# Four indirect row scatters of a batch, issued as two pairs or one by one across two iterations

## The chip, the cores and the metric

The kernel runs on one core of one Trainium2 chip. The metric is the device time of an execution in microseconds; the time before is the median of three runs. One further execution was recorded by the hardware profiler, and the rows shown come from it.

## The reference

One transformer block with adaptive layer norm, for 32 batches of 256 tokens and 128 features: attention with 8 heads, then a mixture of 8 experts of which each token takes 2. Cut to what matters:

```python
h = layernorm(x) * (1 + ca) + sa
x = x + ga * attn(h)            # q, k: rmsnorm and rope; causal softmax; 8 heads of 128
h = layernorm(x) * (1 + cb) + sb
scores = softmax(h @ Wr + br)
_, top_idx = top_k(scores, 2)   # weights: softmax over the chosen two
expert_out = gelu(h @ W1[e] + b1[e]) @ W2[e] + b2[e]
x = x + gb * sum over the two chosen e of weights[e] * expert_out[e]
```

All inputs and outputs are float32.

## The kernel before

The kernel has two stages. In the first, attention and the choice of experts, a software pipeline goes over the 32 batches; in the second the rows of the tokens, sorted by expert in DRAM (`x_rows`), are taken in tiles through the experts' matrices, and their results go back by rows (`y_rows`). Between the stages stand the ends of one block of instruction streams and the start of another.

In the first stage each engine has one written-out stream, `body(half, parity, live)`, called by `iterations` for n = -2 to 33. The iterations n = 8 to 29 are a loop of 11 turns with two iterations in each (parity 0 and 1); those before and after are unrolled. Iteration n works on several batches at once, each at its own step: the layer norm of batch n + 1 (flag X), queries and keys of batch n (A), their transposes and the values of batch n - 1 (B), scores, softmax and values times probabilities of batch n - 2 (C), the gated residual of batch n - 3 (R), the second layer norm of batch n - 4 (N2), the logits and choice of experts of batch n - 5 (RT), and the places and scatters of batch n - 6 (ST). Each engine goes through eight head groups h = 0 to 7, a half of one of four 128 x 1024 products each.

For a head group TensorE (from L1133 on) makes the scores of one head (L1162 to L1165), the product that gives queries or keys (L1129), at h = 0, 1, 5 and 6 eight transposes of an earlier product (L1204), at h = 2 and 3 the values (L1129 again), and then values times probabilities of the head before (L1144 to L1147). The transposes at h = 5 and 6 take the scaled queries; they share one PSUM tensor, UN[1], so those at h = 6 wait until ScalarE has copied those of h = 5 to `q_t` (L733). ScalarE does the exponentials of a head (L690, L692), four squares with sums of the product (L714), which wait for the product, and copies. VectorE divides and adds the heads (L966, L982), multiplies the product by cosine (L1015) and sine (`rope_b`, L1030), and for h = 0 to 3 adds the two (L1039). At h = 3 it sums the places (L950), and at h = 4 it copies the turned rows of batch n - 5 into `rows` (L960), for which it waits until the scatters of batch n - 7, which read the same buffer, have landed.

GpSimd's stream is in the order of the function below: `roots`, `gated_residual`, `newton`, `offsets`, `scale_queries(0)`, the product `place_k`, `scale_queries(1)`, scatter of row tile 0 (two indirect DMAs, one for each chosen expert), the scores of RT, scatter of row tile 1 (two more), `h_lo`, the second weight, and the sums `add(4)` to `add(7)` with small steps of RT between them. An indirect DMA writes 128 rows of 129 float32 values to `x_rows` at the rows that `place` names. `alone` is a wait of its own instruction; in the loop, where its value is not constant, it is a move to a register and two waits.

`rows` and `place` have two buffers each, by the parity of the batch. Batch 27 (LAST - 1) is scattered in the second stage (L1414). SP's stream waits for the scatters of batches 0 to 26 (L426) before it issues the loads of the first three tiles (L430).

Of the kernel before, what the change touches and what calls it, by code (L numbers as in the profile page):

```python
# [19 lines left out]
def adaln_block(nc, x, wq, wk, wv, wo, wr, br, w1, b1, w2, b2, c, wmod, rope_cos, rope_sin, out):  # L20
# [12 lines left out]
    K = 2  # L33
# [13 lines left out]
    LAST = NB - LATE  # L47
# [12 lines left out]
    with ctx:  # L60
# [27 lines left out]
        x_rows = nc.dram_tensor("x_rows", [(E * REGION + SPARE * TILE), RW], F32).ap()  # L88
# [114 lines left out]
        rows = [sb("rows0", [P, K, TT, RW]), rows_kept]  # L203
# [27 lines left out]
        place = [sb("place0", [P, TT * K], I32), place_kept]  # L231
# [203 lines left out]
        def _(pool):  # L435
# [50 lines left out]
            def body(half, parity, live):  # L486
# [79 lines left out]

                def scatter(t):

                    b = n - 6
                    alone(pool, "place_ready", b + 1)  # L570
                    alone(pool, "rows_tagged", b + 1)
                    for j in range(K):
                        at = place[parity][:, t * K + j:t * K + j + 1]
                        pool.indirect_dma_start(  # L574
                            out=x_rows, out_offset=bass.IndirectOffsetOnAxis(ap=at, axis=0),
                            in_=rows[parity][:, j, t, :], in_offset=None).then_inc(S[f"scattered{parity}"], 16)

                if X or A or B or C or R or N2:
                    roots()
                if R:  # L580
                    gated_residual()
                if X or A or B or C or R or N2:
                    newton()
                    offsets()
                if B:
                    scale_queries(0)
# [7 lines left out]
                if B:  # L594
                    scale_queries(1)
                now = ST and not (isinstance(n, int) and n - 6 == LAST - 1)
                if now:
                    scatter(0)
                if RT:
# [4 lines left out]
                                       op=ALU.mult).then_inc(S["scored"], 1)  # L604
                if now:
                    scatter(1)
                if X:
                    b = n + 1
                    wait(pool, "hhi_done", b + 1)
                    wait(pool, "vw_done", TT * (b - 1))  # L610
                    pool.tensor_tensor(out=h_lo[other][:, :], in0=h_t[:, :], in1=h_hi[other][:, :], op=ALU.subtract)\
                        .then_inc(S["h_ready"], 1)
                if ST:
                    b = n - 6
# [5 lines left out]
                if A:  # L620
                    add(4)
                    add(5)
# [1379 lines left out]
```

## Time and profile before

| | us |
|---|---|
| median of 3 runs | 1255.39 |
| lowest and highest | 1252.91, 1262.49 |
| profiled execution | 1272.64 |
| its span, first to last instruction | 1270.7 |

The span is what the profile's rows are measured in: their times are microseconds from its start. Busy times of engines are parts of it. The profiled execution is one run, a little over the range of the three timed ones, so a sum of rows is a sum for that execution, and the median is a second reference. An idle time in square brackets stands before an instruction, with what ended it.

### The profile page before, as it was taken

To read this page: it belongs to the slowest core of one execution; us is meant where nothing else is said; L and a number is where in the kernel's file an instruction comes from. 1 tells how busy PE (TensorE), PEld (TensorE's weight loads), DVE (VectorE), ACT (ScalarE), POOL (GpSimd) and SP (SyncE) were. 2 spreads that over 40 slices of the span, in tenths; PEclk is the share of its full clock that TensorE was granted. 3 is DMA by queue.
4 is the path that set the end of the run, shared out by engine and by line. 5 is a ranking of instruction groups with operands and counts; after the bars stand their busy time and mean duration, and the time that the engine had idled before them with its cause. 6 is when DMAs were issued, how large, how long until landed. Compare 5 with 4: busy or idle time off the path is not lost. (4 is left out here: it accounts for less than half of the span.)

```text
span 1270.7 us, 30656 instructions
## 1 busy us (share of the span) xinstructions
PE 1068.5 (84%) x7431; PEld 805.2 (63%) x7431; DVE 941.6 (74%) x2589; ACT 976.5 (77%) x3518; POOL 791.5 (62%) x1198
## 2 busy tenths in 40 slices
PE   3699999999898899989999998999899679887700
PEld 2278888777777777767777776787654334566500
DVE  2988888888887787878778787887567466565644
ACT  3889998888888887878888787887598458776532
POOL 2556577767666676666667666677446656654543
PEclk9999999999999999999999999999999879998855
DMA  8300000000000000000000000000333232210064
GB/s 261 112 19 5 4 12 12 14 12 19 11 11 11 12 12 11 15 15 11 11 12 12 11 15 15 11 12 16 98 98 93 69 97 80 82 53 23 32 247 150
DMA packets 50769, 57.73 MB, mean 45 GB/s; under 512 B 7868, under 2 KB 38703, under 8 KB 50644
## 3 DMA queue, kind: packets, MB, share of 16 engines
q1 hardware_dynamic: 33492, 35.37, 9.3%
q0 software_dynamic: 8704, 16.87, 4.0%
q10 hardware_dynamic: 8448, 4.20, 1.1%
q14 instruction: 92, 0.75, 0.2%
q8 instruction: 33, 0.54, 0.2%
HBM read 33.21 MB, written 24.23 MB: 45 GB/s over the span
## 5 line engine op out<-in xcount | busy, mean ns | idle before, releaser
L714 ACT ACTIVATE squares<-unit 128x128 f32<-128x128 f32 x1024 | 270.3, 290 | 37.2 <-remote 25.2
L1444 POOL DMA_INDIRECT y_rows<-y_out,place_y x144 | 153.9, 1069 | 121.5 <-DVE y_out L1826 77.2
L714 ACT ACTIVATION_READ_ACCUMULATOR squares<-unit 128x1 f32 x1024 | 226.3, 223 | 0.0
L544 POOL TENSOR_TENSOR roped<-roped,rope_b 128x512 f32<-128x512 f32 x128 | 165.6, 1294 | 97.3 <-DVE rope_b L1030 95.2
L1015 DVE TENSOR_TENSOR roped<-unit,cos_sb 128x512 f32<-128x512 f32 x256 | 175.0, 684 | 57.2 <-ACT squares L714 53.8
L690 ACT ACTIVATE probs<-scores,rr 128x256 f32<-128x256 f32 x256 | 121.5, 475 | 85.2 <-PE scores L1165 53.0
L1204 PE MATMUL unit<-ident,roped 128*128 128x128 f32 x1024 | 139.2, 280 | 53.8 <-ACT q_t L733 39.0
L1204 PEld LDWEIGHTS unit<-ident,roped 128*128 128x128 f32 x1024 | 115.6, 142 | 100.0 <-issue 83.3
L1030 DVE TENSOR_TENSOR rope_b<-unit,sin_sb 128x512 f32<-128x512 f32 x256 | 173.5, 678 | 0.0
L574 POOL DMA_INDIRECT x_rows<-rows,place x108 | 109.9, 1018 | 64.2 <-DVE place L950 42.1
L1039 DVE TENSOR_TENSOR roped<-roped,rope_b 128x512 f32<-128x512 f32 x128 | 141.9, 1109 | 4.4
L982 DVE SCALAR_TENSOR_TENSOR acc<-pv,den,acc 128x128 f32<-128x128 f32 x448 | 135.8, 338 | 0.3
L1531 ACT ACTIVATE hidden<-up,b_t 128x512 f32<-128x512 f32 (+1 forms) x188 | 100.1, 597 | 34.2 <-remote 20.7
L552 POOL TENSOR_TENSOR roped<-roped,rr 128x1024 f32<-128x1024 f32 x64 | 122.0, 1910 | 0.0
L966 DVE RECIPROCAL den<-pv 128x2 f32<-128x2 f32 x256 | 40.5, 158 | 100.3 <-PE pv L1147 62.4
L1129 PE MATMUL unit<-wqk_hi,h_hi 128*128 128x512 f16 x256 | 100.6, 393 | 10.3 <-DVE rope_b L1030 8.4
L1144 PE MATMUL pv<-vals,probs 128*128 128x129 f32 x512 | 104.0, 285 | 0.1
L1129 PE MATMUL unit<-wqk_lo,h_hi 128*128 128x512 f16 x256 | 100.8, 394 | 0.0
L1129 PE MATMUL unit<-wqk_hi,h_lo 128*128 128x512 f16 x256 | 100.3, 392 | 0.0
L1162 PE MATMUL scores<-q_t,k_t 128*128 128x128 f32 x512 | 99.6, 276 | 0.5 <-ACT q_t L733 0.5
L1147 PE MATMUL pv<-vals,probs 128*128 128x129 f32 x512 | 99.8, 277 | 0.0
L1164 PE MATMUL scores<-q_t,k_t 128*128 128x128 f32 x512 | 99.7, 277 | 0.0
(292 smaller groups left out, 3010.9 us busy)
## 6 DMA issues: line engine op xcount, KB each, us to landing
shared<-y_rows SPq DMA_DIRECT2D x16, 512.0 KB, 5.2
x_all<-in_L_attn_x SPq DMA_DIRECT2D x32, 128.0 KB, 2.1
out_x<-sums ACTq DMA_DIRECT2D x16, 256.0 KB, 3.9
rope_b<-x_rows SPq DMA_DIRECT2D x13, 258.0 KB
tile_x<-x_rows SPq DMA_DIRECT2D x12, 258.0 KB
y_rows<-y_out,place_y POOLq DMA_INDIRECT x144
x_rows<-filler SPq DMA_DIRECT2D x16, 129.0 KB
k_t<-in_L_ffn_W SPq DMA_DIRECT2D x2, 1024.0 KB, 10.1
```

The source lines that it names most:

```text
L544: pool.tensor_tensor(out=roped[parity][:, u, heads], in0=roped[parity][:, u, heads], in1=rope_b[:, u % 2, heads], op=ALU.add).then_inc(S[" ...
L552: pool.tensor_tensor(out=v, in0=v, in1=r, op=ALU.mult).then_inc(S["qs_done"], 1)
L574: pool.indirect_dma_start(out=x_rows, out_offset=bass.IndirectOffsetOnAxis(ap=at, axis=0), in_=rows[parity][:, j, t, :], in_offset=None).t ...
L690: nc.scalar.activation(probs[:, h % NPR, 0:T], SC[h % 2][:, 0:T], ACT.Exp, scale=r[:, kc:kc + 1]).then_inc(S["exp_done"], 1)
L714: nc.scalar.activation(squares[:, c * D:(c + 1) * D], UN[0][:, c * D:(c + 1) * D], ACT.Square, accum_out=ssq[parity][:, u * H + c:u * H + ...
L982: ins = nc.vector.scalar_tensor_tensor(out=a[:, t, :], in0=o[:, t, 0:M], scalar=den[:, h % 2, t:t + 1], in1=a[:, t, :], op0=ALU.mult, op1= ...
L1015: nc.vector.tensor_tensor(out=roped[parity][:, u, heads].rearrange("p (g c) -> p g c", c=D // 2), in0=UN[0][:, heads].rearrange("p (g c) - ...
L1030: nc.vector.tensor_tensor(out=rope_b[:, u % 2, heads].rearrange("p (h s c) -> p h s c", h=HH, s=2), in0=UN[0][:, heads].rearrange("p (h s ...
L1039: nc.vector.tensor_tensor(out=roped[parity][:, u, heads], in0=roped[parity][:, u, heads], in1=rope_b[:, u % 2, heads], op=ALU.add).then_in ...
L1129: ins = nc.tensor.matmul(dst[:, k:k + 512], a, w[:, k:k + 512], start=(m == 0), stop=(m == 2))
L1204: ins = nc.tensor.transpose(UN[1][:, j * P:(j + 1) * P], roped[other][:, u, j * D:(j + 1) * D], ident[:, :])
L1444: pool.indirect_dma_start(out=y_rows, out_offset=bass.IndirectOffsetOnAxis(ap=place_y[i % (2 * SLOTS)][:, s:s + 1], axis=0), in_=y_out[at] ...
```

## The change

In GpSimd's stream of the first stage, `scatter` issues one indirect DMA instead of two, and takes the batch, its buffer, the row tile and the expert's number. The four scatters of batch b = n - 6 now stand at four places: the first where the first pair stood, the second behind `add(4)`, the third first in iteration n + 1, ahead of `roots`, and the fourth in iteration n + 1 behind `offsets`. Each has its own pair of waits. `add(4)` comes before the second weight. The number of scatters, what they write and their semaphores' final counts stay. For batch 26 the last two are issued in n = 33.

```diff
-                def scatter(t):
-
-                    b = n - 6
+                def scatter(b, k, t, j):
+
                     alone(pool, "place_ready", b + 1)
                     alone(pool, "rows_tagged", b + 1)
-                    for j in range(K):
-                        at = place[parity][:, t * K + j:t * K + j + 1]
-                        pool.indirect_dma_start(
-                            out=x_rows, out_offset=bass.IndirectOffsetOnAxis(ap=at, axis=0),
-                            in_=rows[parity][:, j, t, :], in_offset=None).then_inc(S[f"scattered{parity}"], 16)
-
+                    at = place[k][:, t * K + j:t * K + j + 1]
+                    pool.indirect_dma_start(
+                        out=x_rows, out_offset=bass.IndirectOffsetOnAxis(ap=at, axis=0),
+                        in_=rows[k][:, j, t, :], in_offset=None).then_inc(S[f"scattered{k}"], 16)
+
+                now = ST and not (isinstance(n, int) and n - 6 == LAST - 1)
+                rest = not isinstance(n, int) or 0 <= n - 7 < LAST - 1
+                if rest:
+                    scatter(n - 7, other, 1, 0)
                 if X or A or B or C or R or N2:
                     roots()
...
                     newton()
                     offsets()
+                if rest:
+                    scatter(n - 7, other, 1, 1)
                 if B:
                     scale_queries(0)
...
                     scale_queries(1)
-                now = ST and not (isinstance(n, int) and n - 6 == LAST - 1)
                 if now:
-                    scatter(0)
+                    scatter(n - 6, parity, 0, 0)
                 if RT:
...
-                if now:
-                    scatter(1)
                 if X:
...
+                if A:
+                    add(4)
+                if now:
+                    scatter(n - 6, parity, 0, 1)
                 if ST:
...
                 if A:
-                    add(4)
                     add(5)
```

## Rows read from the trace of the kernel before

**Rows 1.** The page, busy time and share of the span: TensorE's multiplications.

```profile
PE 1068.5 (84%) x7431; PEld 805.2 (63%) x7431; DVE 941.6 (74%) x2589; ACT 976.5 (77%) x3518; POOL 791.5 (62%) x1198
```

**Rows 2.** Busy time by stretch: length, each engine's busy (instructions), granted clock, DMA share, GB/s.

```profile
143.43:168.12 24.69, 24.69 (x187) 20.34 (x187) 21.78 (x66) 22.74 (x97) 14.99 (x27) 1.00 0.02 5
193.07:217.89 24.82, 24.82 (x189) 20.16 (x188) 21.99 (x70) 22.56 (x98) 18.81 (x32) 1.00 0.05 16
606.53:634.39 27.86, 25.27 (x189) 20.10 (x188) 22.71 (x70) 23.89 (x103) 18.87 (x33) 1.00 0.04 12
634.39:661.27 26.88, 25.20 (x189) 20.11 (x188) 22.50 (x69) 22.09 (x93) 18.87 (x33) 1.00 0.04 13
217.89:828.72 610.83, 559.46 (x4116) 446.10 (x4115) 496.64 (x1519) 506.42 (x2135) 414.91 (x684) 0.99 0.04 13
```

**Rows 3.** Groups of instructions, the loop: count, busy us, mean ns, idle before, what ended it.

```profile
L1039 DVE TENSOR_TENSOR roped<-roped,rope_b 128x512 f32<-128x512 f32 x88 | 98.7, 1122 | 3.0
L1204 PE MATMUL unit<-ident,roped 128*128 128x128 f32 x704 | 94.6, 277 | 51.4 <-ACT q_t L733 39.0 <-ACT k_t L733 11.4
L574 POOL DMA_INDIRECT x_rows<-rows,place x88 | 89.9, 1022 | 54.4 <-DVE place L950 37.4 <-issue 17.0
```

**Rows 4.** Order of time, loop iteration n = 22: start, duration, engine, instruction, idle before.

```profile
619.56 1.04 POOL L574 DMA_INDIRECT x_rows<-rows,place  x1 [1.64 <-DVE place L950]
619.75 0.67 DVE L1030 TENSOR_TENSOR rope_b<-unit,sin_sb 128x512 f32<-128x512 f32 x1
620.90 1.07 POOL L574 DMA_INDIRECT x_rows<-rows,place  x1 [0.30 <-issue]
621.49 0.38 PE L1129 MATMUL unit<-wqk_hi,h_lo 128*128 128x512 f16 x1
622.39 1.01 POOL L574 DMA_INDIRECT x_rows<-rows,place  x1 [0.17 <-issue]
623.71 0.96 POOL L574 DMA_INDIRECT x_rows<-rows,place  x1 [0.30 <-issue]
623.99 0.28 ACT L714 ACTIVATE squares<-unit 128x128 f32<-128x128 f32 x1 [1.52 <-remote]
624.69 0.68 POOL L611 TENSOR_TENSOR h_lo<-h_t,h_hi 128x256 f16<-128x256 f32 x1
626.67 1.09 PE L1204 MATMUL unit<-ident,roped 128*128 128x128 f32 x8 [1.61 <-ACT q_t L733]
```

**Rows 5.** Order of time, unrolled iteration n = 7, GpSimd's scatters and ScalarE's squares.

```profile
204.23 1.04 POOL L574 DMA_INDIRECT x_rows<-rows,place  x1 [0.99 <-DVE place L950]
205.57 0.96 POOL L574 DMA_INDIRECT x_rows<-rows,place  x1 [0.30 <-issue]
207.33 1.01 POOL L574 DMA_INDIRECT x_rows<-rows,place  x1 [0.49 <-issue]
207.72 0.28 ACT L714 ACTIVATE squares<-unit 128x128 f32<-128x128 f32 x1
208.64 0.96 POOL L574 DMA_INDIRECT x_rows<-rows,place  x1 [0.30 <-issue]
```

**Rows 6.** Order of time, loop iteration n = 23: GpSimd, VectorE and ScalarE before the scatters.

```profile
638.22 0.25 POOL L516 TENSOR_TENSOR correction<-guess 128x40 f32<-128x40 f32 x1 [0.68 <-ACT guess L741]
639.97 1.90 POOL L552 TENSOR_TENSOR roped<-roped,rr 128x1024 f32<-128x1024 f32 x1
640.35 2.06 DVE L1039 TENSOR_TENSOR roped<-roped,rope_b 128x512 f32<-128x512 f32 x1
641.62 0.87 ACT L761 ACTIVATE xn<-x_all,off,rr 128x128 f32 x2
645.36 0.16 DVE L950 TENSOR_REDUCE place<-place_k 128x4 int32<-128x32 f32 x1
```

**Rows 7.** Order of time, the end of the first stage: SP's first tile loads, TensorE.

```profile
898.65 2.02 SPq L430 DMA_DIRECT2D rope_b<-x_rows  x3
911.98 0.63 PE L1930 MATMUL xt<-ident,rope_b 128*128 128x128 f32 x4 [2.33 <-PEq L1288]
```

## What the change will do to the time

> **What bounds the kernel now.** I read the page first: TensorE is busy 1068.5 us of the span [rows 1], the most of any engine, and little of it is idle between 60 and 900 us, where attention runs. All the changed code runs there. So the second view is busy time by stretch, cut at GpSimd's first instruction of an iteration (L496) [rows 2]. The reader is to see three lengths. An iteration without scatters takes 24.69 us and TensorE is busy for all of it. The unrolled iteration n = 7, with the same four scatters as the loop's, takes 24.82 and TensorE is again busy throughout. The loop's two iterations take 27.86 and 26.88, with TensorE idle for 2.59 and 1.68. The 22 iterations of the loop take 610.83 us, 27.77 each, and TensorE is idle for 51.4 of them. So the loop is not bound by work: about 3 us an iteration go into a wait.
>
> The groups of instructions in the loop name it [rows 3]: all 51.4 us of idleness stand before the transposes of L1204, 39.0 of it until ScalarE has copied q_t, 11.4 until k_t. The k_t part is at the loop's jump (10 times, only before even n). The q_t part comes in each iteration, 39.0 / 22 = 1.77 us.
>
> The order of time shows where it starts [rows 4]. The product of head group 5 ends on TensorE at 621.49 + 0.38 = 621.87, but ScalarE's squares of it begin at 623.99, after 1.52 us idle "remote", that is, on a signal that came later than the record of the work. The late squares delay the copy of q_t, and TensorE stands for 1.61 us until 626.67. In just these 5 us GpSimd runs its four scatters: starts 619.56, 620.90 (1.34 apart), 622.39, 623.71. In the unrolled iteration [rows 5] the starts are 204.23, 205.57, 207.33, 208.64: the second pair begins 1.76 after the second scatter instead of 1.49, and the squares follow their product without idle time. My reading: while GpSimd issues scatters one upon another, TensorE's signals are held back; where a pause lies between them, the hold ends soon and is hidden. That is an inference from where the idle time lies, not a row.
>
> **The change, part by part.** It adds and removes no scatter: 22 x 4 = 88 in the loop [rows 3], about 1.02 us each, and the rows move the same bytes. It places them (A) first in the iteration, (B) behind offsets, both for the batch before, (C) where the first stood, (D) behind add(4).
>
> (1) The burst goes. Starts become some 6 us apart: A at about 0.2, B at 6.5, C at 12 to 13, D at 17 to 18 us of an iteration. Worth at most the whole q_t wait, 39.0 us; at least nothing, if a lone scatter holds a signal as long.
>
> (2) A before roots. One scatter and its gap, 1.04 + 0.30 = 1.34 us [rows 4], up to 1.8 if its waits are not passed early. It waits for nothing (its batch's rows and places are an iteration old). Behind it stand roots, L560, L565 and newton; in [rows 6] newton begins at 638.22, with 0.68 us of idle time in front of it, so rr and the offsets come 0.5 to 1.1 us later. The scaling at 639.97 begins when they are done; ScalarE wants them for xn at 641.62, 1.6 us on: nothing on the path.
>
> (3) B before scale_queries(0). The scalings, 1.90 us each, start 1.3 to 2.7 us later than at 639.97 in [rows 6], the second ends near 12.5 us of the iteration. TensorE takes the first scaled queries with the transposes of head group 5, at 14 us: hidden, cover 1.5 us or more. place_k slides between the scalings to about 10.5 us; VectorE sums places at 645.36, which is 10.97: cover 0.3 us, the thinnest.
>
> (4) Three pairs of waits more on GpSimd's queue. In the loop the first scatter starts 0.9 us after VectorE's sum of places ended, so one set costs up to 0.75 us where nothing hides it. GpSimd's work is 18.9 us [rows 2]; with four scatter gaps of up to 0.75 it needs 22, under 24.8. After scatter D it does add(5) at 19.3, and add(7) still waits for VectorE. Hidden, but no longer loosely.
>
> (5) h_lo and score come forward: h_lo stood at 624.69 [rows 4] behind four scatters, now behind one. No reader waits for it this early: nothing.
>
> (6) The last two scatters move to n = 33, where B ends near 903. The first tile loads, issued at 898.65 [rows 7], wait for all scatters and go out 6 us later; TensorE's first transpose of a tile is at 911.98, so these loads have some 6 us of cover for the time they need. Nothing; without cover it would be once, not per iteration.
>
> (7) VectorE's sums collide elsewhere with the scalings. L1039 has a mean of 1122 ns in the loop [rows 3] and took 2.06 us at 640.35, beside the scaling of 639.97 to 641.87 [rows 6]: it ended only after it. With B first, this sum is free (1.4 us gained on VectorE, which TensorE does not need), but the next one, now due near 10 us, may meet the second scaling. If it does, the following rope_b slips by up to 1.4 us; its cover is the start of the product of head group 5, 621.49 - 2 x 0.21 = 621.07, less 619.75 + 0.67, that is 0.65 us [rows 4]. Price 0 to 0.8 us an iteration; at four chances in ten I take 0.3.
> The Trainium skill (SBUF — State Buffer, section "SBUF: two separate sides") says why: a VectorE tensor_tensor with both inputs in SBUF and a GpSimd operation exclude each other for the whole instruction; the row agrees.
>
> Sum for an iteration of the loop: 1.77 gained, 0.3 lost, 1.47; by 22, 32 us. The unrolled iterations have nothing to gain, TensorE being full there. The profiled execution took 1272.64 us (span 1270.7) and goes to about 1240. The median of the runs shown, 1255.39, is 17 us lower; the 39 us of waits cannot all be the profiler's then, and I take the same 32 off: 1223.
>
> **Rivals.** (a) Nothing moves. The late signals have another source, or are much shorter in a timed run. For: GpSimd is shown by no row as the releaser; the difference between profiled and timed is of the same order as the waits. Against: [rows 5] has the same work without the wait. Time 1252 to 1259. Chance 0.17.
> By the same section of the skill, TensorE and ScalarE never wait on another engine's or a DMA's access to SBUF; the late signals would then not be the scatters', and the time 1255. The rows show only that they coincide.
>
> (b) The signals improve but VectorE's collision takes most of it: 0.8 to 1.4 us of the 1.77 is lost again. Gain 8 to 21 us, time 1234 to 1247. For: cover 0.65. Against: VectorE begins that stretch 1.4 us earlier. Chance 0.10.
>
> (c) Slower. A lone scatter holds TensorE's signals as long as one in the burst, and there are now four places instead of one; B falls where ScalarE copies vals right after its product. If two of the four cost ScalarE the 1.52 us of [rows 4], that is 3.04 for 1.77: 1.27 x 22 = 28 us, time 1283 (1268 to 1290). It decides once a lone scatter costs the path more than 1.77 / 4 = 0.44 us. For: each scatter's transfer and issue are as before. Against: in [rows 5] four of them, in two pairs, cost TensorE nothing. Chance 0.13.
>
> **How the numbers follow.** The forecast has 0.60: 1223, and its own range is 1255 less the full 39 and some of the jump's 11, that is 1208, up to 1236. Adding (b) and (a) reaches 1260; (c) is left out with some of the lowest end. Range 1207 to 1260. About 1%, 12.5 us, is what a measurement can tell from no change: below 1243 lie the forecast and two thirds of (b), 0.67; within, (a) and the rest of (b), 0.20; above, 0.13.
>
> **What would show it.** In the profile after: loop iterations of 25 to 26.5 us; before L1204 at most 10 us until q_t in all, the k_t part as before; "remote" gone before squares (L714) and den; GpSimd's four scatters 5 us or more apart; L1039's longest cases in other head groups. The sum is wrong if q_t waits stay with scatters apart (a), if they turn into waits of TensorE for rope_b (b), or if new late signals stand beside A, B or D (c).

## The result and the profile after

The changed kernel is faster by about half of what was forecast. Its median is 1245.43 us over 8 runs, against 1261.26 us over 8 runs of the kernel before: a ratio of 0.9889, 95% interval 0.9854 to 0.9924, or 16 us. The forecast was 32 us, to 1223. (The kernel before has a median of 1258 to 1264 us on the chips used below, so each ratio is taken with the runs beside it.)

The profiled execution took 1243.83 us, against 1272.64 before. That difference of 28.8 us is two things, which the table parts. The first stage ends here where TensorE begins the first tile's transpose [rows 7]; the loop is cut at TensorE's first scores of n = 8 and of n = 30. (The windows of [rows 2] and of the stretches below are cut at GpSimd's L496, which comes 1.3 us later against TensorE in after, with a scatter ahead of it. The loop's length is the same within 0.1 us by either cut.)

| profiled execution, us | before | after | difference |
|---|---|---|---|
| first stage up to the loop (n = 8) | 214.7 | 215.4 | +0.7 |
| the 22 iterations of the loop | 610.8 | 588.2 | -22.6 |
| from the loop to the first tile | 86.4 | 90.5 | +4.1 |
| first stage | 912.0 | 894.1 | -17.9 |
| second stage | 358.7 | 347.8 | -10.9 |

No changed line runs in the second stage, and in the twelve profiles of this study it took 346.6 to 358.7 us, with before and after near the two ends. The 10.9 us are its own spread. The 17.9 us of the first stage are what the change did, and they agree with the 16 us timed.

Busy time by stretch, kernel after (length, then each engine's busy time and instructions in the order TensorE, its weight loads, VectorE, ScalarE, GpSimd, then the granted clock, DMA share, GB/s). The stretches are n = 7, n = 22, n = 23, the loop, and the second stage:

```profile
194.10:219.90 25.80, 25.04 (x188) 19.99 (x187) 22.36 (x70) 22.89 (x98) 19.08 (x32) 1.00 0.05 15
594.20:621.30 27.10, 25.70 (x191) 20.66 (x192) 23.86 (x73) 23.92 (x102) 19.02 (x32) 1.00 0.04 12
621.30:647.50 26.20, 24.77 (x185) 19.71 (x183) 22.09 (x67) 22.08 (x95) 18.96 (x31) 1.00 0.05 14
219.72:807.98 588.26, 557.95 (x4119) 447.03 (x4118) 503.24 (x1519) 507.96 (x2136) 418.32 (x683) 0.99 0.04 13
894.10:1241.90 347.80, 239.30 (x1456) 150.46 (x1456) 212.43 (x411) 226.61 (x398) 197.42 (x186) 0.85 0.32 99
```

Against [rows 2], the loop is 22.6 us shorter. TensorE's idle time there fell from 51.4 to 588.26 - 557.95 = 30.3 us, which is 21.1 of it. But the unrolled n = 7 is 1.0 us longer, where nothing had been waited for before.

Groups of instructions in the loop of after:

```profile
L1043 DVE TENSOR_TENSOR roped<-roped,rope_b 128x512 f32<-128x512 f32 x88 | 106.9, 1215 | 3.0
L1208 PE MATMUL unit<-ident,roped 128*128 128x128 f32 x709 | 94.2, 276 | 23.3 <-DVE rows L964 11.3 <-ACT k_t L737 11.1
L1133 PE MATMUL unit<-wqk_hi,h_hi 128*128 128x512 f16 x176 | 67.4, 383 | 7.0 <-DVE rope_b L1034 7.0
```

Lines from `scatter` on stand up to four further down in the changed file: L1208, L1133, L1043 and L964 are L1204, L1129, L1039 and L960 of before. In [rows 3] TensorE's transposes waited 39.0 us for ScalarE's q_t. That wait is gone altogether. Two waits for VectorE stand in its place: 11.3 us until it has copied `rows` (L964), and 7.0 until it has written `rope_b` (L1034), together 18.3. The wait for k_t at the loop's jump is as before, 11.1 beside 11.4.

In order of time, iteration n = 22 of after (compare [rows 4, 6]):

```profile
593.11 1.01 POOL L572 DMA_INDIRECT x_rows<-rows,place  x1 [0.18 <-issue]
600.13 1.23 POOL L572 DMA_INDIRECT x_rows<-rows,place  x1 [0.65 <-issue]
601.40 1.90 POOL L552 TENSOR_TENSOR roped<-roped,rr 128x1024 f32<-128x1024 f32 x1
603.03 2.88 DVE L1043 TENSOR_TENSOR roped<-roped,rope_b 128x512 f32<-128x512 f32 x1
603.25 0.25 POOL L595 TENSOR_TENSOR place_k<-one_hot,place_e 128x32 f32<-128x32 f32 x1
603.46 1.90 POOL L552 TENSOR_TENSOR roped<-roped,rr 128x1024 f32<-128x1024 f32 x1
606.99 1.01 POOL L572 DMA_INDIRECT x_rows<-rows,place  x1 [1.64 <-DVE place L954]
607.92 0.39 PE L1133 MATMUL unit<-wqk_hi,h_hi 128*128 128x512 f16 x1 [0.35 <-DVE rope_b L1034]
608.58 0.67 DVE L964 COPY rows<-unit 128x512 f32<-128x512 f32 x1
609.31 1.09 PE L1208 MATMUL unit<-ident,roped 128*128 128x128 f32 x8 [0.57 <-DVE rows L964]
612.53 1.01 POOL L572 DMA_INDIRECT x_rows<-rows,place  x1 [0.16 <-issue]
```

The four scatters are 5.5 to 7 us apart, and no signal comes late beside any of them: where VectorE waits for a product beside a scatter, `den` starts 0.04 us behind the product's end, as elsewhere. The second one pushes the two scalings (L552) to 601.40 and 603.46. VectorE's sum of head group 2 starts at 603.03 and ends at 605.91, 0.55 us after the second scaling has ended: 2.88 us, where a sum of the same shape takes 0.69 us undisturbed. Everything that VectorE does next is late, `rope_b` and then the copy of `rows`, and TensorE stands 0.35 us for the one and 0.57 for the other.

### The profile page after: what moved, and what is told of

Read it like the earlier page. It is cut to its first block and busy times, and to the rows that moved or that the text cites. A ratio compares the mean times of both kernels' runs of the same rounds, so it can differ in the third digit from the quotient of the medians.

```text
span 1241.9 us, 30842 instructions
## 1 busy us (share of the span) xinstructions
PE 1061.9 (86%) x7431; PEld 805.2 (65%) x7431; DVE 951.8 (77%) x2589; ACT 979.0 (79%) x3518; POOL 797.9 (64%) x1198
## 5 line engine op out<-in xcount | busy, mean ns | idle before, releaser
L544 POOL TENSOR_TENSOR roped<-roped,rope_b 128x512 f32<-128x512 f32 x128 | 166.1, 1297 | 100.8 <-DVE rope_b L1034 99.0
L718 ACT ACTIVATION_READ_ACCUMULATOR squares<-unit 128x1 f32 x1024 | 222.8, 219 | 0.0
L1034 DVE TENSOR_TENSOR rope_b<-unit,sin_sb 128x512 f32<-128x512 f32 x256 | 173.6, 678 | 0.0
L1208 PE MATMUL unit<-ident,roped 128*128 128x128 f32 x1024 | 138.0, 279 | 27.5 <-DVE rows L964 13.8
L1208 PEld LDWEIGHTS unit<-ident,roped 128*128 128x128 f32 x1024 | 117.2, 142 | 68.3 <-DVE rows L964 25.8
L1043 DVE TENSOR_TENSOR roped<-roped,rope_b 128x512 f32<-128x512 f32 x128 | 150.8, 1178 | 4.4
L552 POOL TENSOR_TENSOR roped<-roped,rr 128x1024 f32<-128x1024 f32 x64 | 122.1, 1911 | 0.8
L1133 PE MATMUL unit<-wqk_hi,h_hi 128*128 128x512 f16 x256 | 100.2, 391 | 18.6 <-DVE rope_b L1034 16.6
L1148 PE MATMUL pv<-vals,probs 128*128 128x129 f32 x512 | 104.1, 285 | 0.1
L1133 PE MATMUL unit<-wqk_lo,h_hi 128*128 128x512 f16 x256 | 100.0, 391 | 0.0
L1133 PE MATMUL unit<-wqk_hi,h_lo 128*128 128x512 f16 x256 | 99.7, 389 | 0.0
L1151 PE MATMUL pv<-vals,probs 128*128 128x129 f32 x512 | 99.5, 276 | 0.0
L1149 PE MATMUL pv<-vals,probs 128*128 128x129 f32 x512 | 99.5, 276 | 0.0
```

Source lines behind the costliest of these rows:

```text
L544: pool.tensor_tensor(out=roped[parity][:, u, heads], in0=roped[parity][:, u, heads], in1=rope_b[:, u % 2, heads], op=ALU.add).then_inc(S[" ...
L552: pool.tensor_tensor(out=v, in0=v, in1=r, op=ALU.mult).then_inc(S["qs_done"], 1)
L718: nc.scalar.activation(squares[:, c * D:(c + 1) * D], UN[0][:, c * D:(c + 1) * D], ACT.Square, accum_out=ssq[parity][:, u * H + c:u * H + ...
L1034: nc.vector.tensor_tensor(out=rope_b[:, u % 2, heads].rearrange("p (h s c) -> p h s c", h=HH, s=2), in0=UN[0][:, heads].rearrange("p (h s ...
L1043: nc.vector.tensor_tensor(out=roped[parity][:, u, heads], in0=roped[parity][:, u, heads], in1=rope_b[:, u % 2, heads], op=ALU.add).then_in ...
L1133: ins = nc.tensor.matmul(dst[:, k:k + 512], a, w[:, k:k + 512], start=(m == 0), stop=(m == 2))
```

## The experiments

The theory tested: the q_t wait comes from the burst of scatters, and half of what its removal gives is taken back by the second scatter, which stands ahead of the scalings and makes VectorE's sum meet them. The rivals: the q_t wait is the profiler's or another cause's; and what is lost comes from the first or fourth scatter, or from batches' scatters reaching into the next iteration. Each sum below is of the loop's 22 iterations, n = 8 to 29, in the profile.

### All four in their own iteration

From after: the third and fourth scatters stand behind `add(5)` and ahead of `add(7)` of their batch's iteration.

```diff
-                if rest:
-                    scatter(n - 7, other, 1, 0)
                 if X or A or B or C or R or N2:
...
-                if rest:
-                    scatter(n - 7, other, 1, 1)
                 if B:
                     scale_queries(0)
...
                     add(5)
+                if now:
+                    scatter(n - 6, parity, 1, 0)
...
+                if now:
+                    scatter(n - 6, parity, 1, 1)
                 if A:
                     add(7)
```

> All four scatters one by one, but all in their own iteration: where the first pair stood, behind add(4), behind add(5), behind the counts ahead of add(7). Nothing stands before the query scalings. Theory 1 (the scatters' burst held TensorE's signals back, and in the changed kernel the shifted scalings blocked VectorE's sum at head group 2): no idle time before the transposes until q_t and none until the rows' copy, L1043's counterpart at about 2 us at most, loop iterations of 24.8 to 26, that is 25.7 on average (26.74 in the changed kernel, 27.77 before), a span about 20 us under the changed kernel's. Rival (TensorE's waits of the changed kernel come from scatters as such, wherever they stand): about 0.9 us per iteration stay, loop iterations of 26.7. Timed: theory 1 1220 to 1232, rival 1243 to 1250.

Measured: 1223.88 us against 1258.36, ratio 0.9700 (0.9642 to 0.9757). The loop and its transposes:

```profile
215.61:786.20 570.59, 551.94 (x4117) 445.37 (x4116) 491.25 (x1519) 504.36 (x2135) 416.45 (x683) 1.00 0.04 14
L1207 PE MATMUL unit<-ident,roped 128*128 128x128 f32 x704 | 93.6, 276 | 18.7 <-ACT k_t L736 10.9 <-POOL roped L544 7.7
```

The loop is 17.7 us shorter than in after. No `rows` and no q_t wait is left. A new one, 7.7 us for GpSimd's sum of an earlier product (L544), shows that GpSimd's later work is not free either; two scatters now stand ahead of its last sum, which is the likely reason. So scatters apart are worth the forecast's gain and more, as long as none stands ahead of the scalings.

### The second pair behind `h_lo`

From before: both pairs stay whole, and only one 0.68-us instruction is put between them.

```diff
-                if now:
-                    scatter(1)
                 if X:
...
                         .then_inc(S["h_ready"], 1)
+                if now:
+                    scatter(1)
```

> The kernel before with one step moved: the low part of the layer norm (0.68 us) stands between the two pairs of scatters instead of behind them, so the second pair starts later after the first. Theory 1 (a third scatter on the heels of the second prolongs the hold): the wait for q_t before the transposes, 39.0 us in the loop, falls under 8 us and a loop iteration takes 25.7 to 26 us, as nothing else was moved. Rival (the place in the iteration decides, not the spacing): it stays at 35 to 40 us and 27.7 us an iteration. Timed: 1225 to 1235 against 1250 to 1262.

Measured: 1228.67 us against 1258.36, ratio 0.9761 (0.9713 to 0.9808).

```profile
214.88:785.60 570.72, 557.66 (x4117) 444.00 (x4115) 493.01 (x1519) 506.01 (x2135) 413.83 (x683) 1.00 0.05 14
L1204 PE MATMUL unit<-ident,roped 128*128 128x128 f32 x704 | 93.6, 276 | 10.2 <-ACT k_t L733 9.2
619.54 1.09 POOL L574 DMA_INDIRECT x_rows<-rows,place  x1 [0.30 <-issue]
621.66 1.01 POOL L574 DMA_INDIRECT x_rows<-rows,place  x1 [0.17 <-issue]
```

The last two lines are the second and third scatter of an iteration: 2.12 us from start to start, where the kernel before had 1.49 [rows 4]. That alone ends the q_t wait, 39.0 us to none, with the four still begun within 4.8 us. The loop gains 40.1 us and the timed median 29.7. Nothing has to be set apart one by one, and nothing moved to the next iteration. The late signals are not all gone: in each iteration ScalarE's exponentials of a head, beside the second pair, start 0.7 to 0.8 us behind the end of their scores, where 0.2 is usual. TensorE does not wait for them here.

### The next iteration's second scatter behind the scalings

From after: one scatter moves by two scalings and `place_k`.

```diff
                     offsets()
-                if rest:
-                    scatter(n - 7, other, 1, 1)
                 if B:
                     scale_queries(0)
...
                     scale_queries(1)
+                if rest:
+                    scatter(n - 7, other, 1, 1)
                 if now:
```

> The changed kernel with one of its scatters moved: the one behind the offsets stands behind the second query scaling, so that the scalings start 1.3 to 2 us earlier. Theory 1: VectorE's sum at head group 2 falls from 2.88 us to about 1, TensorE's waits for the rows' copy (13.0 us between 200 and 870) and for rope_b before the product (7.6 us) fall under 5 us together, loop iterations lose about 0.9 us (26.74 to 25.8). That scatter then stands 1.4 to 2 us ahead of the next, a pair; if pairs hold signals too, up to 0.6 us of this is not seen. Rival (these waits come from the scatter first in the iteration): unchanged.

Measured: 1230.07 us, one execution, against 1258.36. The loop, its transposes, and VectorE's sum of head group 2 in an iteration:

```profile
215.50:783.05 567.55, 552.87 (x4116) 445.31 (x4115) 493.31 (x1519) 503.64 (x2135) 422.61 (x683) 1.00 0.04 14
L1208 PE MATMUL unit<-ident,roped 128*128 128x128 f32 x704 | 93.6, 276 | 14.7 <-ACT k_t L737 11.0 <-DVE rows L964 2.6
614.77 0.99 DVE L1043 TENSOR_TENSOR roped<-roped,rope_b 128x512 f32<-128x512 f32 x1
```

This is the run that decides the place of the loss. The scatter ahead of `roots` and the one behind `add(4)` stayed where the change put them, and the loop fell by 20.7 us against after. The sum takes 0.99 us instead of 2.88, the wait for `rows` 2.6 us instead of 11.3, and the wait for `rope_b` is gone. It also has two scatters next to each other, behind the scalings, and no q_t wait.

### The second pair behind `add(4)`

From before: the pair moves further, past `h_lo`, the second weight and `add(4)`.

```diff
                     add(4)
+                if now:
+                    scatter(1)
+                if A:
                     add(5)
```

> The kernel before with its second pair of scatters behind add(4), 4 us or more after the first pair. Theory 1, in its narrow form (it takes a third scatter on the heels of the second): no wait for q_t, loop iterations of 25.7 to 26. In its wide form (any second scatter on the heels of a first holds signals for 1.5 us): 20 us or more of waits until q_t or of late signals stay in the loop, 26.5 us and more an iteration.

Measured: 1238.33 us, one execution, against 1258.36. From the loop's windows and its waits (us in total, times, longest):

```profile
216.75:791.38 574.63, 555.69 (x4117) 445.76 (x4116) 488.90 (x1519) 505.62 (x2135) 415.14 (x683) 1.00 0.04 14
PE pv L1145 <- DVE acc L983: 13.8, 22, 0.7
```

Again no q_t wait. But the 574.6 us are 26.1 an iteration, a little over the narrow form's range, and TensorE waits 13.8 us for VectorE's `acc` in a place where the other kernels have no such wait. The order of time shows why:

```profile
604.71 0.39 PE L1148 MATMUL pv<-vals,probs 128*128 128x129 f32 x2
604.91 0.96 POOL L574 DMA_INDIRECT x_rows<-rows,place  x1 [0.30 <-issue]
606.40 0.17 DVE L967 RECIPROCAL den<-pv 128x2 f32<-128x2 f32 x1 [1.58 <-PE pv L1148]
608.04 0.46 PE L1145 MATMUL pv<-vals,probs 128*128 128x129 f32 x2 [0.63 <-DVE acc L983]
```

The product ends on TensorE at 604.71 + 0.39 = 605.10. VectorE, idle for it, begins `den` at 606.40, 1.3 us later, while the pair's second scatter runs; `acc` and TensorE follow late. In all 22 iterations this `den` starts 1.24 to 1.34 us behind its product. So a pair of scatters 1.3 us apart holds signals too, for a shorter time than four in a row, and at this place TensorE's path needs one of them. The expectation's wide form is right in that and wrong on the size, and its narrow form, that it takes a third scatter, falls.

### All four in a row behind `h_lo`

From before: the burst is not parted but moved.

```diff
                         .then_inc(S["h_ready"], 1)
+                if now:
+                    scatter(0)
+                if now:
+                    scatter(1)
```

> The kernel before with all four scatters behind the layer norm's low part, 1.34 us apart throughout, some 2.5 us later in the iteration. Theory 1 (three and more scatters on each other's heels hold TensorE's signals back wherever they stand): late signals again, 20 us and more in the loop of idle time until a signal later than its work's record, now at head groups 5 to 7; loop iterations of 26.5 us and more. Rival (the place in the iteration decides): none, and 25.7 to 26 us.

Measured: 1307.76 us, one execution, against 1264.05: the slowest kernel of the study. The loop's window, and three of its waits (us in total, times, longest):

```profile
218.98:859.72 640.74, 575.43 (x4116) 458.80 (x4115) 492.10 (x1521) 502.00 (x2135) 411.64 (x683) 0.97 0.04 12
PE unit L1244 <- ACT q_t L733: 59.1, 22, 2.8
DVE den L966 <- remote: 52.8, 22, 2.6
ACT probs L690 <- remote: 44.0, 17, 2.9
```

The four start 1.26 to 1.34 us apart. The late signals ("remote") moved with them, from the squares of head group 5 to later readers of TensorE's products, on VectorE and on ScalarE alike, and the longest are 2.6 to 2.9 us. With the same four DMAs of the same rows in each iteration, the loop takes 570.7 us with 2.12 us in the middle of them and 640.7 with 1.3 throughout. That ties the long late signals to the burst: they went with it to another place, and a pause in its middle takes them away. Not all of the 70 us are waits. TensorE's idle time went from 13.1 to 65.3 us, and its own busy time from 557.7 to 575.4, at a mean granted clock of 0.97 beside 1.00.

### `place_k` ahead of both scalings

From the version with the second pair behind `h_lo`: the scalings start late, as in after, but through `place_k` and not through a scatter.

```diff
                     offsets()
-                if B:
-                    scale_queries(0)
                 if ST:
                     b = n - 6
...
                                        op=ALU.mult).then_inc(S["place_k_done"], 1)
                 if B:
+                    scale_queries(0)
+                if B:
                     scale_queries(1)
```

> The kernel of the run with the layer norm's low part between the pairs of scatters, with one more step moved: the product place_k stands ahead of both query scalings, so it waits for VectorE's place_e and both scalings start 1.5 to 3 us later, about where they stand in the changed kernel, while no scatter moves. Theory 1 (the shifted scalings cost the changed kernel its 0.9 us an iteration): VectorE's sum at head group 2 takes 2.5 us or more, TensorE waits for rope_b before the product and for the rows' copy, and the loop goes from 570.7 back to 585 to 592 us. Rival (scatters in the middle of GpSimd's stream cost it): it stays at 571 to 574.

Measured: 1235.32 us, one execution, against 1264.05; the loop 578.3 us, less than was expected. Loop, transposes, the two scalings and the sum:

```profile
215.70:794.04 578.34, 556.26 (x4116) 448.21 (x4115) 469.16 (x1520) 505.60 (x2135) 422.51 (x683) 0.99 0.04 13
L1204 PE MATMUL unit<-ident,roped 128*128 128x128 f32 x704 | 93.5, 276 | 22.1 <-ACT k_t L733 12.4 <-issue 8.7
621.08 4.20 POOL L552 TENSOR_TENSOR roped<-roped,rr 128x1024 f32<-128x1024 f32 x2
622.65 0.88 DVE L1039 TENSOR_TENSOR roped<-roped,rope_b 128x512 f32<-128x512 f32 x1
```

The sum comes at the same moment as in after, 12.4 us behind TensorE's first scores of the iteration, while a scaling runs. But here it is let in between the two scalings and takes 0.88 us, and the second scaling stretches instead: the two take 4.20 us where 1.90 each would be 3.8. No wait for `rows` follows, and the loop lies between the ranges of the theory (585 to 592) and of the rival (571 to 574). So it isn't enough that the sum meets the scalings; it must also be passed over. The 8.7 us of "issue" are a wait for q_t, by the order of time:

```profile
626.82 0.39 PE L1165 MATMUL scores<-q_t,k_t 128*128 128x128 f32 x2
628.41 0.47 ACT L690 ACTIVATE probs<-scores,rr 128x256 f32<-128x256 f32 x1 [0.79 <-PE scores L1165]
```

The scores end at 627.21, and ScalarE's exponentials start 1.2 us later, beside the first pair's second scatter (626.79 to 627.75). ScalarE then goes on without idle time to the copy of `q_t` (630.04 to 631.10), and TensorE's next transposes begin at 631.22 after 0.40 us idle, the same in all 22 iterations.

### The second scatter between the scalings

From after: one scatter moves past the first scaling only.

```diff
-                if rest:
-                    scatter(n - 7, other, 1, 1)
                 if B:
                     scale_queries(0)
+                if rest:
+                    scatter(n - 7, other, 1, 1)
                 if ST:
```

> The changed kernel with the scatter behind the offsets put between the two query scalings: the first scaling starts as early as before, VectorE can make its sum beside the scatter. Theory 1: the sum at head group 2 takes at most 1.2 us, no waits for the rows' copy or rope_b, loop 563 to 570 us (588 in the changed kernel), timed about 1220 to 1228, 2.5 to 3 per cent under the kernel before. Rival (the scatters cost it): loop 585 and more, timed 1240 to 1250.

Measured: 1244.68 us against 1264.05, ratio 0.9845 (0.9815 to 0.9875); the loop 582.0 us, against an expectation of 563 to 570. A miss. Loop, transposes, and VectorE's sums of head groups 1 and 2:

```profile
215.46:797.49 582.03, 556.90 (x4116) 446.87 (x4115) 505.66 (x1519) 506.11 (x2135) 422.30 (x683) 0.99 0.04 13
L1208 PE MATMUL unit<-ident,roped 128*128 128x128 f32 x704 | 93.5, 276 | 23.3 <-DVE rows L964 11.3 <-ACT k_t L737 11.0
622.07 2.34 DVE L1043 TENSOR_TENSOR roped<-roped,rope_b 128x512 f32<-128x512 f32 x1
626.36 1.62 DVE L1043 TENSOR_TENSOR roped<-roped,rope_b 128x512 f32<-128x512 f32 x1
```

The first scaling meets the sum of head group 1 (2.34 us), as it does in before (2.06) [rows 6]. The scatter between the scalings then makes the second scaling late enough to meet the sum of head group 2 too (1.62 us). VectorE pays 1.65 and 0.93 us over an undisturbed 0.69 and TensorE waits 11.3 us for `rows` again. Moving the scatter out of the scalings' way wants both of them passed, as in the run that put it behind both (loop 567.6 us).

### Three in their own iteration, one in the next

From after: the third scatter goes behind `add(5)`, the fourth alone stands first in the next iteration.

```diff
                 if rest:
-                    scatter(n - 7, other, 1, 0)
+                    scatter(n - 7, other, 1, 1)
...
-                if rest:
-                    scatter(n - 7, other, 1, 1)
...
                     add(5)
+                if now:
+                    scatter(n - 6, parity, 1, 0)
```

> Three scatters one by one in their own iteration (where the first pair stood, behind add(4), behind add(5)) and only the fourth first in the next. Theory 1: neither late signals nor the collision, and not the wait for the last sum that the kernel with all four in their own iteration has (10.7 us between 200 and 860): loop 563 to 567 us, timed 1218 to 1226. Rival (the one first in the iteration delays GpSimd's sums): loop over 570.

Measured: 1223.45 us against 1264.05, ratio 0.9687 (0.9658 to 0.9717). This is the fastest version found, level with the first experiment's. Loop, transposes and the sum of head group 2:

```profile
214.61:782.65 568.04, 552.83 (x4116) 445.35 (x4115) 493.57 (x1519) 503.03 (x2135) 416.01 (x683) 1.00 0.04 14
L1208 PE MATMUL unit<-ident,roped 128*128 128x128 f32 x704 | 93.5, 276 | 15.2 <-ACT k_t L737 11.5 <-DVE rows L964 2.8
614.64 0.99 DVE L1043 TENSOR_TENSOR roped<-roped,rope_b 128x512 f32<-128x512 f32 x1
```

It has the change's idea, lone scatters and one carried into the next iteration, without the scatter ahead of the scalings, and it takes 20.2 us less for the loop than after. A scatter first in an iteration is free, as the prediction's step (2) had it.

### The same delay without a scatter

From the version with the second pair behind `h_lo`: in the loop, four small fills of a spare buffer, each waiting for the last, stand ahead of the first scaling.

```diff
                     offsets()
+                if not isinstance(n, int):
+                    for k in range(4):
+                        alone(pool, "idle_done", 4 * (n - 8) + k + 1)
+                        pool.memset(filler[:, :, 0:M], 0.0).then_inc(S["idle_done"], 1)
                 if B:
                     scale_queries(0)
```

> The kernel with the layer norm's low part between the pairs (loop 570.7 us, no late signals), its scatters where they are, plus four small fills of 0.3 us on GpSimd, each waiting for the last, ahead of the first query scaling, in the loop only. They move both scalings and place_k back by about 2 us, in the order first scaling, place_k, second scaling, as the fourth scatter does in the changed kernel, without a scatter in the middle. Theory 1: VectorE's sum at head group 2 takes 2.5 us or more again, TensorE waits for the rows' copy and for rope_b, and the loop takes 586 to 592 us. Rival (the scatter itself costs TensorE something there, or the shift is harmless, as the run with place_k first suggests): 570 to 579 us.

Measured: 1245.34 us, one execution, against 1263.95. (Some 9 us of the total are lost ahead of the loop, where the fills' buffer is waited for, so the loop is what is to be read.)

```profile
223.76:805.14 581.38, 559.53 (x4116) 447.47 (x4115) 484.98 (x1517) 504.75 (x2135) 442.83 (x771) 0.99 0.04 13
626.96 1.61 POOL L590 MEMSET filler<- 128x256 f32 x4
628.53 1.90 POOL L554 TENSOR_TENSOR roped<-roped,rr 128x1024 f32<-128x1024 f32 x1
L1210 PE MATMUL unit<-ident,roped 128*128 128x128 f32 x704 | 93.6, 276 | 19.9 <-ACT k_t L739 11.3 <-issue 6.9
```

1.61 us of fills in the place of a scatter cost the loop 581.4 - 570.7 = 10.7 us. The direction is the theory's; the size is under its range and over the rival's. In the 11 iterations of odd n the sum of head group 2 starts 0.04 us after the second scaling has, and takes 2.40 us, and TensorE stands 0.57 us before the transposes of head group 5 until the copy of `rows` has ended (it begins 0.04 us behind it; the profile puts these 6.2 us down to "issue"). In 8 of the other 11 the sum comes in between the scalings and takes 0.7 us, with no such wait. No DMA has been moved or added, so a loss at this place does not need one. Only 6.2 of the 10.7 us are seen at it; 2.1 more are in the wait for k_t and 1.9 in TensorE's busy time.

### `place_k` behind both scalings

From after: the scalings follow each other directly.

```diff
                 if B:
                     scale_queries(0)
+                if B:
+                    scale_queries(1)
                 if ST:
...
-                if B:
-                    scale_queries(1)
```

> The changed kernel with place_k (0.25 us) behind the second query scaling instead of between the two. In the run with place_k first, VectorE's sum came in between two scalings that follow each other directly and took 0.88 us; in the changed kernel it was passed over twice, by place_k and by the second scaling, and took 2.88. Theory 2 (two operations of GpSimd with a third behind them in its queue keep VectorE out, a direct pair lets it in): the sum at head group 2 takes about 1 us, the waits for the rows' copy fall under 5 us, loop 568 to 575 us, timed 1225 to 1232. Rival (the sum loses whenever it begins late in the first scaling): it stays at 2.5 us or more and the loop at 585 to 590; place_k, now later, makes it rather longer.

Measured: 1248.10 us against 1263.95, ratio 0.9875 (0.9820 to 0.9930).

```profile
216.03:805.19 589.16, 556.49 (x4117) 445.42 (x4115) 503.59 (x1519) 507.04 (x2135) 428.52 (x683) 1.00 0.04 13
L1208 PE MATMUL unit<-ident,roped 128*128 128x128 f32 x704 | 93.6, 276 | 24.4 <-DVE rows L964 11.9 <-ACT k_t L737 11.5
```

The loop is as long as in after, 589.2 beside 588.3. The idea that the sum is passed over because `place_k` stands between the scalings falls: without it the sum was passed over too (2.6 to 3.0 us) in each of the loop's 21 iterations in which it started inside the first scaling.

### What the runs say together

From the starts in each trace, for iteration n = 23, in us from TensorE's first scores of that iteration: when the scalings start, the sum of head group 2, when VectorE's copy of `rows` starts, and how long the iteration is.

| version | scalings | sum: start, took | copy of rows | iteration |
|---|---|---|---|---|
| second pair behind `h_lo` | 8.72, 11.67 | 13.12, 0.99 | 16.78 | 25.45 |
| three and one | 9.02, 11.98 | 13.43, 0.99 | 17.09 | 25.37 |
| second scatter behind the scalings | 9.04, 11.99 | 13.44, 0.99 | 17.10 | 25.38 |
| four fills | 10.29, 12.36 | 12.40, 2.40 | 17.47 | 25.79 |
| second scatter between | 9.02, 12.60 | 13.43, 1.62 | 17.72 | 26.00 |
| after | 10.75, 12.81 | 12.39, 2.87 | 17.94 | 26.22 |
| after, `place_k` last | 10.74, 12.59 | 12.39, 2.66 | 17.97 | 26.25 |

Up to a copy at 17.1 the iteration takes 25.4 us. From there it grows by as much as the copy is late: 17.94 - 17.10 = 0.84 later, 26.22 - 25.38 = 0.84 longer, and the four versions in between or beside lie on the same line within 0.05. Different edits, one reader: the transposes of head group 5, which go into the bank that the copy of `rows` must have read. Where VectorE is in time, the copy has 17.10 - 16.78 = 0.32 us of cover.

Three versions stand outside the table: all four in their own iteration (17.38, 25.66), the second pair behind `add(4)` (16.78, 25.92) and `place_k` ahead (16.46, 25.55). Each has another wait of its own, named above: `roped`, and `acc` and `q_t` behind a late signal beside a pair. The first of them lies on the line although TensorE never waits for `rows` in it, so the line alone would not name the reader; the profile's own waits for `rows` do.

## Why the prediction was right in its mechanism and wrong in its size

**What bounded the kernel, and step (1), the burst:** right. The q_t wait went from 39.0 us to none, with 88 scatters of 1.02 to 1.03 us in either kernel. "Remote" is gone before the squares and before `den`. The inference that the argument rested on, that the hold is tied to scatters one upon another and ends where a pause lies between them, is borne out by the two runs that kept all four together, with a pause (loop 570.7) and without (640.7). It is not the whole of it: pairs hold signals by some 0.6 to 1.4 us as well. In n = 7 of before [rows 5] an exponential starts 0.55 us behind its scores beside the second pair, and TensorE does not wait for it.

**Steps (2), (4), (5), hidden:** right. Newton's wait for ScalarE took up the scatter ahead of `roots`: it began at 597.60 with 0.72 us of idle time before it, as in [rows 6]. No new wait for GpSimd's queue stands in after's groups.

**Step (6), the tile loads:** wrong by some 2.5 us, once. By the clock the loads went out 14 us earlier, but TensorE's last multiplication of the stage ended 20.4 us earlier (889.21 instead of 909.66), so against it they went out 6.8 us later, much as the prediction said:

```profile
884.96 2.02 SPq L430 DMA_DIRECT2D rope_b<-x_rows  x3
894.08 1.09 PE L1934 MATMUL xt<-ident,rope_b 128*128 128x128 f32 x4 [4.88 <-PEq L1292]
```

TensorE's idle time before the first tile grew from 2.33 us [rows 7] to 4.88. It is 4.8 to 5.1 us in the four versions whose last scatter stands behind the offsets or later in n = 33, and 2.2 to 2.3 in the other eight. What the second block of streams waits for there is not shown.

**Step (3):** its readers' covers held (the scaled queries are not waited for, nor the sum of places), but its real effect is in (7).

**Step (7), VectorE's sum and the second scaling: this term was mis-sized.** The mechanism stood there as the prediction put it: the sum of head group 2 meets the second scaling and the following `rope_b` slips. It took 0.3 us an iteration, from a price of 0 to 0.8 at four chances in ten. Measured are 18.3 / 22 = 0.83 us of TensorE's idle time, a little over the top of that range. Three things went into that:

- *The chance, which is the most of it.* The meeting is the rule: the sum took 2.8 us or more in 20 of the loop's 22 iterations. The prediction's own times pointed to it: with the second scaling ending near 12.5 us, it begins near 10.6, and the sum was due near 10. At its full price the term would have been 0.75 instead of 0.3.
- *The reader.* The prediction followed only `rope_b` to the product of head group 5, and there the wait is 7.0 us. Next on VectorE's queue is the copy of `rows`, with 0.32 us of cover instead of 0.65, and there stands the larger one, 11.3 us. It was read as a wait for GpSimd's scatters alone, and not as an instruction for which TensorE waits.
- *The slip, which was under its price.* The sum itself loses more than the 1.4 us assumed, 2.88 - 0.69 = 2.19, since it starts before the first scaling has ended and is passed over at its end. But it also starts 0.73 us earlier (12.39 instead of 13.12), so what comes behind it slips by 17.94 - 16.78 = 1.16 us. Less the copy's 0.32 that is 0.84, the price measured.

With what was measured, 1.77 - 0.83 = 0.94 us an iteration, or 20.7 us for 22. The loop became 22.6 shorter; TensorE's busy time fell by 1.5 of the rest.

**"The unrolled iterations have nothing to gain":** true, and not the whole of it. They have the same sums and the same scalings, no late signals to be rid of, and so they lose. n = 7, 30 and 31 went from 24.8 to between 25.7 and 25.9 us each, 2.9 in all. With the 2.5 us of step (6) that is 5.4, and the table has 0.7 + 4.1 = 4.8 us outside the loop; the difference is within the spread of what nothing changed (n = 5 begins at 142.9 to 144.2 us in these kernels, the one with the fills left out). A step that costs where nothing is gained belongs in the sum. So of the 14 us by which the first stage's gain stayed under the forecast, some 10 are in the loop, by term (7), and some 5 outside it.

**Profiled against timed:** right. The waits are not the profiler's. Timed gain beside the first stage's: after 16 and 17.9 us, the second scatter between the scalings 19.4 and 23.7, all four in their own iteration 34.5 and 38.2, three and one 40.6 and 43.6, `place_k` last 15.9 and 13.1. Only the second pair behind `h_lo` has a wider gap, 29.7 timed beside 40.0, and why is open.

**Rivals.** (a) falls: the q_t wait went, and the time followed. (c) falls: no late signal stands beside a lone scatter in after. (b), at a chance of 0.10, is what happened: 0.83 us lost again is in its 0.8 to 1.4, and 1245 us in its 1234 to 1247. What was held against it, that VectorE begins that stretch 1.4 us earlier, is true of the sum of head group 1 (0.69 us instead of 2.06) and is part of the trouble: the sum of head group 2 came 0.73 us earlier, into the end of the first scaling, which came 2.0 us later, and so the whole second one passed before it.

## What to carry to other kernels

Before a stall is priced by its own length, follow the instruction that slips down its engine's queue and list every reader of each thing behind it; the thinnest cover counts, not the first. Where four DMAs of one engine must only not stand in a row, one instruction between the pairs may do what moving each of them does: one `h_lo` between them brought 0.9761, the change as made 0.9889. Then look who waits for TensorE beside each pair: a pair behind `add(4)` cost 13.8 us of waits, the pairs here none. Where moving them one by one is wanted, keep them behind the work whose results others share a port or a queue with: the same idea with no scatter ahead of the scalings gives 0.9687.

## What the runs showed of the hardware

**Indirect DMAs in a row hold back TensorE's signals.** With four issued by GpSimd at 1.26 to 1.51 us from start to start, ScalarE and VectorE stood idle for up to 2.9 us before products that TensorE's records show as ended; VectorE's `den` started 1.75 to 2.3 us behind its product in every iteration of both such loops. With two at 1.3 us (the runs with pairs), a reader beside the second started 0.6 to 1.4 us behind, where 0.03 to 0.2 is usual. In the runs whose scatters are all 1.6 us or more apart, none that waited was over 0.5 us behind. What holds the signals was not found. By the Trainium skill (SBUF — State Buffer, section "SBUF: two separate sides") TensorE and ScalarE never wait on another engine's port, nor a DMA on an engine's. No run here contradicts that for data; the rule is on ports, and what came late here are signals of finished work.

**A VectorE sum can be passed over.** With both inputs in SBUF it doesn't end while a GpSimd scaling runs: in after and in `place_k` last it ended 0.55 to 0.57 us behind the second scaling, which is what the same section of the Trainium skill states as an exclusive lock. That section of the Trainium skill also gives the lock to whichever starts first. In after the sum had started before the first scaling ended (by 0.27 us at n = 22), and GpSimd's next instructions still went ahead of it, in all 20 iterations of the loop in which it started there; with `place_k` ahead of both scalings it was let in between them, in all 22. Who gets in at such a boundary stays open: the one explanation tried, the instruction between the scalings, fell.

**Also open:** why TensorE waits for k_t at the loop's jump, 9 to 12 us in ten of the twelve kernels (4.2 with the second pair behind `add(4)`, 4.9 with all four in a row), which none of these edits was aimed at.
